# A six-layer transformer chain on one NeuronCore: quantised weights made by fewer vector steps, their sums formed on TensorE, and the weight norms moved into the first feed-forward stage

## The reference, cut to what matters

```python
def ternary_quant(w_fp32, g=64):
    w = w_fp32.astype(bfloat16)
    w_g = w.reshape(-1, g)
    scale = clip(mean(abs(w_g), axis=-1, keepdims=True), 1e-08, None)
    q = clip(round(w_g / scale), -1, 1)
    w_hat = (q * scale).reshape(w.shape)
    return w + stop_gradient(w_hat - w)
def ffn(x, w_gate_up, w_proj):           # 2048 x 256 and 256 x 1024 weights
    gate, up = split(x @ ternary_quant(w_gate_up).T, 2)
    h = silu(gate) * up
    return rms_norm(h) @ ternary_quant(w_proj).T
x = x + 0.5 * ffn(layernorm(x), w_gate_up, w_proj)
x = x + attention(layernorm(x), w_qkv, w_out)       # and four more stages
```

## Time and profile before

| | before |
|---|---|
| median of the runs | 1758.96 us |
| profiled execution, its own time | 1759.25 us |
| span of its instructions | 1757.4 us |
| PE / DVE / ACT / POOL busy | 94% / 73% / 69% / 64% |
| first `up` matmul | 50.87 us |
| first `squares` matmul | 73.64 us |
| last `squares` of the first stage | 147.81 us |

### The profile page before, as it was taken

One profiled execution on the slowest core, in us unless ns is written; L12 is line 12 of the kernel. 1 busy time (PEld: TensorE's weight loads), 2 busy tenths in 40 slices (PEclk: granted clock), 3 DMA queues, 4 the chain that ended last, 5 costly groups with the idle time before them and its releaser, 6 DMA issues.

```text
span 1757.4 us, 26693 instructions
## 1 busy us (share of the span) xinstructions
PE 1646.9 (94%) x9307; PEld 966.0 (55%) x9307; DVE 1287.9 (73%) x2427; ACT 1219.9 (69%) x1886; POOL 1126.6 (64%) x747
## 2 busy tenths in 40 slices
PE   0898789999999999999999999998999999899998
PEld 0565345555555555555555555554565565676565
DVE  7878667777777777777777777785687778886766
ACT  6655778888888988988988888874554443325432
POOL 0555778888888888888888888873663222653222
PEclk9999899999999999999999999999999999999999
DMA  8100667887888878878888788784001210000001
GB/s 284 49 1 19 112 114 140 139 143 143 147 149 151 145 132 166 142 136 161 139 141 150 132 144 154 128 137 81 0 1 58 64 40 1 1 1 28 28 10 48
DMA packets 580506, 174.03 MB, mean 99 GB/s; under 512 B 543243, under 2 KB 579350, under 8 KB 580246
## 3 DMA queue, kind: packets, MB, share of 16 engines
q1 hardware_dynamic: 580374, 172.33, 51.5%
HBM read 35.94 MB, written 2.10 MB: 22 GB/s over the span
## 4 chain that ended last, share of the span: by engine, by line
PE 73%; DVE 8%; POOL 2%; issue 2%; ACT 1%; SPq 0%; DMA 0%; DVEq 0%; POOLq 0%; ACTq 0%
PE banks L1794 23%; PE banks L1795 23%; PE banks L1796 23%; DVE X L1649 1%; POOL sq_sum L684 1%; DVE mo_h L1636 1%; DVE nmax L1466 1%; DVE x L1199 1%; PE banks L1860 1%; PE banks L1892 1%; PE banks L1804 1%; PE banks L1861 1%; PE banks L1893 0%; PE banks L1944 0%; PE banks L2105 0%
## 5 line engine op out<-in xcount | busy, mean ns | idle before, releaser
L737 POOL TENSOR_TENSOR Pl<-Pm,Ph 128x1024 f16<-128x1024 f32 x256 | 546.3, 2134 | 55.6 <-ACT Ph L962 54.4
L952 ACT ACTIVATE Pm<-banks,nbias,s_scale 128x1024 f32<-128x1024 f32 x256 | 308.0, 1203 | 127.7 <-DVE nbias L1468 127.7
L1466 DVE TENSOR_REDUCE nmax<-banks 128x1 f32<-128x1024 f32 x256 | 312.6, 1221 | 113.2 <-PE banks L1796 112.1
L962 ACT ACTIVATE Ph<-Pm 128x1024 f16<-128x1024 f32 x256 | 268.3, 1048 | 1.3
L716 POOL TENSOR_TENSOR rp_b<-rp_s,rope 128x512 f32<-128x512 f32 x128 | 162.8, 1272 | 149.4 <-ACT rp_s L929 149.3
L1505 DVE SCALAR_TENSOR_TENSOR X<-banks,rinv,X 128x256 f32<-128x256 f32 x256 | 112.7, 479 | 157.2 <-PE banks L1796 157.2
L790 POOL TENSOR_TENSOR mT_lo<-mo_h,mT_hi 128x512 f16<-128x512 f32 x72 | 83.7, 1163 | 214.2 <-ACT mT_hi L1067 213.9
L1794 PE MATMUL banks<-QK_hi 128*128 128x512 f16 x512 | 196.6, 384 | 7.5 <-DVE QK_lo L1544 4.3
L1794 PE MATMUL banks<-PT_hi,V_hi 128*128 128x512 f16 x512 | 195.1, 381 | 3.2 <-DMA PT_lo<-Pl 3.2
L1796 PE MATMUL banks<-QK_hi,QK_lo 128*128 128x512 f16 x512 | 195.6, 382 | 0.0
L1795 PE MATMUL banks<-QK_lo,QK_hi 128*128 128x512 f16 x512 | 195.6, 382 | 0.0
(11 more groups left out here) (240 smaller groups left out, 4152.5 us busy)
## 6 DMA issues: line engine op xcount, KB each, us to landing
moe_raw<-in_L_ffn_W SPq DMA_DIRECT2D x72, 128.0 KB, 2.4
w_all<-in_L_attn_w_qkv SPq DMA_DIRECT2D x3, 2048.0 KB, 16.5
a_raw<-in_L_attn_w_qkv SPq DMA_DIRECT2D x24, 256.0 KB, 3.1
PT_hi<-Ph SPq DMA_TRANSPOSE x256, 3.4
PT_lo<-Pl SPq DMA_TRANSPOSE x256, 3.4
raw_gu<-in_L_ffn_w_gate_up SPq DMA_DIRECT2D x2, 1024.0 KB, 7.1
X<-in_L_attn_x SPq DMA_DIRECT2D x2, 1024.0 KB, 12.9
o_raw<-in_L_attn_w_out SPq DMA_DIRECT2D x8, 256.0 KB, 3.5
```

The lines of the kernel that those rows point to most:

```text
L737: nc.gpsimd.tensor_tensor(Pl[:, z % 4, :], Pm[:, k, :], Ph[:, z % 4, :], ALU.subtract).then_inc(pl_done.sem, 1)
L952: nc.scalar.activation(Pm[:, k, :], two_banks[z % 2][:], ACT.Exp, bias=nbias[:, z:z + 1], scale=s_scale[:], accum_out=rsum[:, z:z + 1]).th ...
L962: nc.scalar.activation(Ph[:, z % 4, :], Pm[:, (base * SLOTS + z) % 3, :], copy).then_inc(ph_done.sem, 1)
L1466: nc.vector.tensor_reduce(nmax[:, z:z + 1], two_banks[z % 2][:], AX, ALU.max, negate=True).then_inc(max_done.sem, 1)
```

## The change

- **Loads.** The three weight loads go first, then the four constant tables, x and the rest.
- **Quantising.** ACT makes 2|w| (same instruction with a scale of 2) and, in place of the sign, spreads each group's bf16 scale over its 64 elements (`scaled`). DVE: group sum, one instruction for the scale (two before, and no threshold), then four full-size steps in place of five: mask 2|w| > scale (both operands now full bf16 tiles), `signed` (sign bits of two bf16 values at a time, on 1024 32-bit words, and-or in one SCALAR_TENSOR_TENSOR), mask times signed value, difference. The sum w + difference is no longer formed by DVE: PE puts two matmuls with the identity into one PSUM block (`transposed_sum`), so that 96 matmuls stand for 48 transposes, and the blocks in PSUM are f32.
- **Order.** Parts 0 and 1 are done one after the other; layer norm of the first tokens lies between them. Part 2's |w| and bf16 copy come in the middle of the gate/up blocks on ACT; its `scaled` behind the first silu, its group sum ahead of the first product on DVE, its four DVE steps behind the products of the steps 0 to 3; its 32 matmuls behind PE's step 5, its copies ahead of step 6. The second half of the layer norm moves from ahead of and inside the steps 0 to 3 to the steps 4 to 8. PE's first `up` waits for the router weights' copy and gate/up blocks 0 to 4 (ACT) and 5 (DVE), not for all copies.
- **Two gate/up blocks** (5 and 7) are copied by DVE, not ACT.
- **POOL_LO** of the first phase is (1, 2, 4, 5, 6), in the others (2, 4, 6) as before; this holds for both feed-forward stages.
- **Norms.** The squares of `w_all` are 12 pieces (128x1024) instead of 3 (128x4096): two inside setup, five in the steps 0 to 4 of phase 1 and five in those of phase 2. DVE sums them at phase 2, step 6; the matmul with ones stands ahead of the down matmuls behind phase 3, step 2; the guard is at phase 3, step 4, POOL's power at step 5, the scales and the split of the router weights (before: phase 0, step 6) on DVE at step 6. SP loads the attention's first tables once the twelve pieces are done.
- Statistics of the second batch's first half: eight in phase 1 instead of four in phase 0 and four in phase 1.

```diff
         def _(sp):
+            for i in range(2):
+                sp.dma_start(of_part(raw, i)..., w_gu[i * FF:(i + 1) * FF]...).then_inc(w_in[i].sem, 16)
+            sp.dma_start(raw[1][:]..., w_proj...).then_inc(w_in[2].sem, 16)
             sp.dma_start(ident[:], t_ident).then_inc(consts_in.sem, 16)
...
-            sp.wait_ge(w_squared.sem, 4)
+            sp.wait_ge(w_squared.sem, 1 + SQ_PIECES)
...
         def _(act):
+            def scaled(i):
+                act.wait_ge(quant_step[i].sem, 2)
+                to, scale = of_part(q_scaled, i), of_part(q_scale, i)
+                nc.scalar.activation(to, scale.unsqueeze(2).broadcast_to([P, scale.shape[1], GROUP]), copy).then_inc(w_scaled[i].sem, 1)
+            doubled_abs(0)
+            doubled_abs(1)
+            scaled(0)
+            bf16_of(0)
+            bf16_of(1)
+            act.wait_ge(consts_in.sem, 96)
+            nc.scalar.activation(identb[:], ident[:], copy).then_inc(identb_made.sem, 1)
+            scaled(1)
...
             for i, (c, r0) in enumerate(SETUP_GU):
+                if i in GU_BY_V:
+                    continue
+                if i == N_GU // 2:
+                    doubled_abs(2)
+                    bf16_of(2)
+                    ln_hi(0, 0, 0)
+                    act.wait_ge(setup_copied.sem, 1)
+                    nc.scalar.activation(gwT_hi[:], gwT[:], ACT.Square, accum_out=w_sq[:, 3:4]).then_inc(w_squared.sem, 1)
+                    for piece in range(SQ_FIRST):
+                        weights_squared(piece)
...
                 for s in range(NS):
+                    if (f, s) == (0, 6):
+                        down_weights(1)
+                        down_weights(3)
+                    if (f, s) == (0, 7):
+                        ln_hi(0, l, 1)
                     silu(s)
+                    if (f, s) == (0, 0):
+                        scaled(2)
                     if s:
                         hi(s - 1)
                         square(s - 1)
+                    if f == 0 and (phase, ht) in SQ_AT:
+                        weights_squared(SQ_FIRST + SQ_AT.index((phase, ht)))
...
         def _(dve):
+            def mask(i):
+                dve.wait_ge(w_scaled[i].sem, 1)
+                nc.vector.tensor_tensor(part(i, 0, q_mask), part(i, 0, q_abs2), part(i, 0, q_scaled), ALU.is_gt).then_inc(quant_step[i].sem, 1)
+            def signed(i):
+                dve.wait_ge(w_bf16[i].sem, 1)
+                nc.vector.scalar_tensor_tensor(words(part(i, 0, q_signed)), words(part(i, 0, q_w)), SIGN_BITS, words(part(i, 3, q_scaled)),
+                                               ALU.bitwise_and, ALU.bitwise_or).then_inc(quant_step[i].sem, 1)
-            def straight_through(i):
-                nc.vector.tensor_tensor(part(i, 0, q_out), part(i, 0, q_w), part(i, 8, q_diff), ALU.add).then_inc(quant_step[i].sem, 1)
+            group_scale(0)
+            group_scale(1)
+            mask(0)
+            signed(0)
+            quantised(0)
+            difference(0)
             dve.wait_ge(x_in[0].sem, 16)
             for t in range(TPH):
                 ln_statistics(0, 0, t)
             ln_variance(0, 0, 0)
+            mask(1)
+            ln_normalise(0, 0, 0)
+            signed(1)
+            quantised(1)
+            difference(1)
             ln_lo(0, 0, 0)
+            for i in GU_BY_V:
+                dve.wait_ge(setup_T.sem, 1 + i + 1)
+                nc.vector.tensor_copy(WguT[:, c, r0 * P:(r0 + 4) * P], bank[SETUP_BANK[i % 4]]).then_inc(setup_copied_v.sem, 1)
+            group_scale(2)
...
+                    if (f, s) == (0, 6):
+                        down_weights(0)
+                        down_weights(2)
+                        ln_normalise(0, l, 1)
+                    if (f, s) == (0, 7):
+                        ln_lo(0, l, 1)
                     product(s)
+                    if f == 0 and s < 4:
+                        (mask, signed, quantised, difference)[s](2)
+                    if (f, s) == (0, 4):
+                        for t in range(TPH, TT):
+                            ln_statistics(0, l, t)
+                        ln_variance(0, l, 1)
...
+                    if f == 0 and phase == 2 and ht == 6:
+                        norm_sums()
+                    if f == 0 and phase == 3 and ht == 4:
+                        norm_guarded()
+                    if f == 0 and phase == 3 and ht == 6:
+                        scales()
                         gate_weights_split()
...
         def _(pe):
+            def transposed_sum(to, groups, i):
+                for n, q in enumerate((q_w, q_diff)):
+                    last = nc.tensor.matmul(to, q[i][:, groups:groups + 2, :].rearrange("p g k -> p (g k)"), identb[:], start=n == 0, stop=n == 1)
+                return last
             for i, (c, r0) in enumerate(SETUP_GU):
-                if i == 4:
-                    pe.wait_ge(w_squared.sem, 4)
-                    nc.tensor.matmul(bank[5][:, 0:4], ones_all[:], w_sq[:], start=True, stop=True).then_inc(w_norm_psum.sem, 1)
+                if i == N_GU // 2:
+                    transpose_x(0, 0, 0)
...
                 if f == 0:
-                    pe.wait_ge(setup_copied.sem, N_SETUP_ACT)
-                    pe.wait_ge(setup_copied_v.sem, N_SETUP_V)
+                    pe.wait_ge(setup_copied.sem, 1 + 5)
+                    pe.wait_ge(setup_copied_v.sem, 1)
...
+                    if (f, s) == (0, 5):
+                        for i in range(N_WP):
+                            down_weights(i)
...
+                    if (f, phase, j) == (0, 2, 0):
+                        pe.wait_ge(w_squared.sem, 2 + SQ_PIECES)
+                        nc.tensor.matmul(bank[4][:, D:D + 4], ones_all[:], w_sq[:, 0:4], start=True, stop=True).then_inc(w_norm_psum.sem, 1)
+                    if (f, phase, j) == (0, 2, 2):
+                        pe.wait_ge(w_norm_made.sem, 1)
```

More of the change, by code:

```diff
@@ L125, in build_program @@
     rstd = sb("rstd", [P, B, TT], f32)
-    w_sq = sb("w_sq", [P, 4], f32)
+    w_sq = sb("w_sq", [P, 4 + SQ_PIECES], f32)
+    identb = sb("identb", [P, P], bf16)
+    ones_all = sb("ones_all", [P, P], f32)
     w_norm = sb("w_norm", [P, 4], f32)
@@ L194, in build_program, with q_tiles @@
     top_ffn = place["at"]
+    NG_GU, NG_P = 2 * FF * D // P // GROUP, D * FF // P // GROUP
+    hT_half = FT * HALF * 4
+    def q_tiles(name, dt, of_gu, of_p):
+        tiles = []
+        for part, groups, at in (("gu", NG_GU, of_gu), ("p", NG_P, of_p)):
+            place["at"] = at
+            tiles.append(sb(f"{name}_{part}", [P, groups, GROUP] if dt is not f32 or "raw" in name else [P, groups], dt))
+        return tiles
+    KB = 1024
+    raw = q_tiles("raw", f32, phase0, hT_at + hT_half)
+    q_scaled = q_tiles("q_scaled", bf16, sq_at + 8 * KB, hT_lo_at + hT_half)
+    q_w = q_tiles("q_w", bf16, sq_at, hT_at + hT_half + 8 * KB)
+    q_abs2 = q_tiles("q_abs2", bf16, hT_lo_at, hT_at + hT_half + 12 * KB)
+    q_mask = q_tiles("q_mask", bf16, hT_lo_at + 8 * KB, hT_lo_at + hT_half + 4 * KB)
+    q_signed, q_what, q_diff = q_scaled, q_mask, q_scaled
+    place["at"] = max(sq_at + 16 * KB, top_ffn)
+    gw_raw = sb("gw_raw", [NE, D], f32)
+    q_sum, q_scale = ([sb(f"{n}{i}", [P, g], dt) for i, g in enumerate((NG_GU, NG_P))] for n, dt in (("q_sum", f32), ("q_scale", bf16)))
+    top_setup = place["at"]
+    assert phase0 + 16 * KB <= hT_at + hT_half and hT_lo_at + 16 * KB <= sq_at
     place["at"] = phase0
@@ L300, in build_program @@
     SQUARES_AFTER = 2
-    POOL_LO = (2, 4, 6)
-    N_POOL_LO = len(POOL_LO)
+    POOL_LO = [(1, 2, 4, 5, 6), (2, 4, 6), (2, 4, 6), (2, 4, 6)]
+    N_POOL_LO = sum(len(hts) for hts in POOL_LO)
     END_BANKS = [(4, 6, 7, 5), (4, 2, 3, 5)]
     def lo_by_pool(s):
-        return s // FT * N_POOL_LO + sum(ht < s % FT for ht in POOL_LO)
+        return sum(k % FT in POOL_LO[k // FT] for k in range(s))
     SLOTS = 2 * TT
@@ L865, in _, with down_weights @@
                 act.wait_ge(setup_T.sem, 1 + i + 1)
-                nc.scalar.activation(WguT[:, c, r0 * P:(r0 + 4) * P], bank[SETUP_BANK[i % 4]].bitcast(bf16)[:, 0:HALF],
+                nc.scalar.activation(WguT[:, c, r0 * P:(r0 + 4) * P], bank[SETUP_BANK[i % 4]],
                                      copy).then_inc(setup_copied.sem, 1)
-            for i in range(1, N_WP, 2):
+            def down_weights(i):
                 act.wait_ge(setup_T.sem, 1 + N_GU + i + 1)
-                nc.scalar.activation(WpT[:, 2 * i:2 * i + 2, :].rearrange("p a d -> p (a d)"), bank[SETUP_BANK[i]].bitcast(bf16)[:, 0:HALF],
-                                     copy).then_inc(setup_copied.sem, 1)
+                nc.scalar.activation(WpT[:, 2 * i:2 * i + 2, :].rearrange("p a d -> p (a d)"), bank[4 + i], copy).then_inc(setup_copied.sem, 1)
@@ L1243, in difference @@
-            def difference(i):
-                dve.wait_ge(w_bf16[i].sem, 1)
```

(25 more changed lines are left out.)

203 lines of the change are left out of this document (100 added, 103 removed).

## The result

The changed kernel takes 1762.19 us in the median of 22 runs (1756.95 to 1766.04), the kernel before 1758.5 in 22 runs beside it (1753.63 to 1761.11). The ratio is 1.0025, 95% interval 1.0014 to 1.0035: slower by about 4 us, and the interval excludes a ratio of 1. The forecast was 1753.1 with a range of 1746.5 to 1759.0. The profiled execution took 1763.39 us, its span is 1761.6 (before 1757.4).

A forecast was written before the change was run, and what follows sets the result against it. PE was taken to bound the whole span, but DVE setup and nearly all of phase 0. Terms -18.3 + 9.0 + 0.7 + 2.8 = -5.8 us gave 1753.1 us, range 1746.5 to 1759.

The forecast's parts named there:

- Term 1: Setup: PE's first `up` matmul comes at 32.6 instead of 50.87, -18.3 us (bounds -19.6 and -16.5).
- Term 2: Phase 0, first `up` to first `squares`: deferred work returns on DVE with POOL contention, +9.0 us (bounds +5.5, +13).
- Term 3: Phases 1 and 2: ACT's added squares pieces and doubled statistics mostly fit in slack, +0.7 us (0 to +3).
- Term 4: Phase 3 and stage end: scales wait for POOL's power, the router split delays product 31, +2.8 us (bounds +0.5, +4.5).
- The second stage at 0: Second feed-forward stage, counted in the rest behind attention: same instructions, so no change, 0 us.
- Attention within 1.7: Attention: same instructions, cost 0, though the clock's dip near 196 us can fall otherwise, +-1.7 us.
- C: Rival: setup work returns whole in phase 0 with 7 us contention, nothing saved, +0.4 us, 1759; chance 0.18.
- D: Rival: thinly spread phase 0 matmuls keep TensorE at its lower clock, +5.5 us, 1764.5; chance 0.08.
- B: Rival: DVE and POOL fit together in phase 0 without contention, -12.4 us, 1746.5; chance 0.24.

The follow-up runs named there:

- e4: Changed kernel plus twenty unused 512-column matmuls where PE would wait for the normalised x in phase 0; 1761.04 us, ratio 1.0015 to the kernel before.
- e1: Changed kernel with DVE's guard of the norms behind step 3 of phase 3 instead of step 4; 1754.14 us, ratio 0.9978 to the kernel before.
- e2: Changed kernel with guard behind step 3 and POOL's power of the norms behind step 3 instead of 5, phase 3; 1752.87 us, ratio 0.9971 to before.
- e6: Changed kernel with guard and POOL's power moved earlier, second-stage POOL_LO as before, and layer norm's second half earlier; 1746.90 us, ratio 0.9945 to before.
- e7: e6 with the router weights' split moved from phase 3, step 6 to behind the stage's last adds; 1750.69 us, ratio 0.9965 to the kernel before.
- e3: Changed kernel with POOL_LO (2, 4, 6) in all phases of the second feed-forward stage only; 1757.44 us, ratio 0.9996 to the kernel before.
- e5: Changed kernel with layer norm's second half earlier in phase 0: statistics at step 0, normalising at step 4; 1756.82 us, ratio 1.0007 to before.
- e9: Changed kernel with part 2 quantised before the first `up` and layer norm's second half where it stood before; 1764.03 us, ratio 1.0038 to before.
- e10: e9 plus guard and POOL's power moved earlier and POOL_LO (2, 4, 6) in every phase of both stages; 1755.06 us, ratio 0.9988 to before.

## Why the prediction was wrong, step by step

- **Term 1** held and was beaten: 31.44 against 32.6. Both unknowns (`signed` 1.2, loads at 6.6) were as taken. The surplus is DVE's shorter way to `difference(1)`, done at 28.2 and not 29.1, mostly because POOL's first power took 1.93 us and not 3.0.
- **Term 2** had the right mechanism and was mis-sized: +12.4 for +9.0, inside its bounds of +5.5 to +13. Its contention (3.0) came in larger operations than the rows of before showed: the normalising +1.6, quantising and difference +0.5 each, two variance operations +1.0 each, one lo +1.1, a mean +0.5. Those alone are 6.1, so the 0 to 7 held and the value chosen was too low. PE's wait that follows was implied (x's second half holds `up(8)`), and the low clock behind it, 1.8 to 2.5 us by e4, was priced only as an all-or-nothing rival.
- **Term 3** held: +0.6.
- **Term 4 is the step that failed:** +9.0 for +2.8. The prediction followed only the late consumers of the norm, `w_root` and product 31; these did come (DVE waited 2.13 for POOL's power, product 31 at 145.83 for 147.0). It did not cost the second wait that the diff adds, PE's `down(2, 2)` on `w_norm_made`, nor ask what stands ahead of the guard in DVE's list. That wait measured 3.97 us, and with the low clock behind it it is the greater part of the term: e1 gives 8 us back by moving the guard alone, e2 has 24.11 us for 31.03, and +2.1 against before is what remains. The split of the router weights, priced at 2.4, took 0.46 in the changed kernel; in e6 it took 2.36, and e7 got 1.7 of that back.
- **The second stage at 0** was wrong: it is +2.1 in the profiles. The shared list POOL_LO accounts for 0.4 to 1.1 of that, 3.4 us more of low clock for the rest. "Same instructions" held for attention, not for it.
- **Attention within 1.7** held here (-0.6), by luck: its length is 1069.2 to 1074.3 us in the twelve profiles other than e1's, of kernels that have the same instructions there (before 1073.1, after 1072.5). The differences are low clock: 10.2 to 20.5 us of it by windows of 1 us, and the length less half of that is 1063.8 to 1064.2 in ten of the twelve and 1062.9 in the other two, the kernel before and e7, which have no split of the router weights in phase 3.
- **The rivals.** C, which put the time back at 1759 by contention and term 4, comes closest in mechanism; none had PE waiting for the guard. D named the clock and came closest in size (1764.5 for 1762.2), by luck, as it had not the place: the clock fell behind single waits of 4 to 5 us, and the first seven steps ran at 216 ns. B fell.

Summed for the profiles: -19.4 + 12.4 + 0.6 + 9.0 - 0.6 + 2.1 + 0.1 = +4.2.

What stays open is the sharing-out of the medians. By ratios to before, e2, e3 and e5 are worth 9.5, 5.1 and 3.2 us against the changed kernel, 17.8 together, and e6, which has all of them, 14.1; each of these carries about 3 us of uncertainty by the intervals, so that the parts don't add up is not shown. The clock in attention's first 80 us is low in other places in each kernel, and one kernel's runs spread over 2 to 12 us, largely with it: e2's four slowest have a mean clock of 0.985 to 0.987 and take 1756.5 to 1757.9, its four fastest 0.991 to 0.993 and 1749.7 to 1751.1. What decides where the clock falls in attention stays open.

## What to carry to other kernels

When a small operation is moved, list for each of its semaphores who waits on it, and for its place what stands ahead of it in its engine's list; a 0.15 us guard behind a contended 3.4 us one held PE for 3.97 us and cost the change its gain. Price an idle of PE of several microseconds above its length, since the matmuls behind it may run at half the clock: here 1.8 to 2.5 us more for one of 5. Before comparing two profiles, sum the low-clock time of each, over the whole stage and not in a fixed window. And a table shared by two stages has to be costed in both.

## What the hardware showed that was not expected

- DVE's stretch beside POOL depends on the instruction and is larger than before's rows suggested: four normalisings 1.38 alone, 2.96, 3.37 and 4.71 beside POOL; a 4-element operation 0.15 and 1.23; the bf16 quantising 1.23 and 1.69. The statistics (1.39 for four at 46.29, with POOL busy) and the products from PSUM (0.68) did not stretch. The Trainium skill, "GPSIMD Engine Reference", section "8. Key points", names two SBUF inputs, or a certain mode of the instruction, as what contends; by these rows the trace agrees for the lo parts, the quantising and the variance operation of 48.35, which read two, and for the statistics, which read one. The normalising and the 4-element operation of 49.62 read one tile and did stretch; whether they ran in that mode no row shows.
- The clock fell behind PE's waits of 5.02, 3.97 and 3.87 us, and also behind ones of 2.16 (before the last down group), 2.54 and 2.03 (e9's and e10's squares 1). It stayed up behind ones of 0.71 and 1.14, and behind one of 2.04 in e6's phase 0. At the 2.7 ahead of the second stage's first squares it fell during the wait or within 3 us behind it in four profiles, and in e9 only 12 us later.
- The granted column doesn't have all of it: in the changed kernel it reads 1.00 in 28 to 30, where matmuls of 128 columns start every 107 ns; e2, at the same spacing, reads 0.50 there.
- 128-column bf16 matmuls with new weights each time start every 107 ns at the lower level and every 55 at the higher, where two 512-column ones are 216 apart.
